# First attention of a two-layer macaron block: the products that sum the softmax totals, and the steps behind them, one loop unit later

## The chip, the cores and the metric

The kernel runs on one core of a Trainium2 chip. The metric is the device time of one execution in microseconds (us); of several runs the median counts. TensorE (PE in the profile) does matrix products, VectorE (DVE), ScalarE (ACT) and GpSimd (POOL) work elementwise, SyncE (SP) issues DMAs. Each engine works through its own queue in order, and engines wait for each other by semaphores.

## The reference

The input x is 2 batches of 1024 tokens of width 128. Six stages add to it in turn: a feed-forward layer with 4-bit weights and activations, attention A, the same feed-forward layer, a mixture-of-experts layer, attention B, and the mixture of experts again. The change touches only attention A:

```python
q, k, v = x @ Wq.T, x @ Wk.T, x @ Wv.T          # 16 heads of 64
sim = 50.0 * tanh((q @ k.T) * 64 ** -0.5 / 50.0)
sim = where(causal, sim, lowest)
attn = softmax(sim, axis=-1)                     # exp(sim) / its sum over the keys
x = x + (attn @ v) @ Wo.T
```

Since the tanh bounds sim to 50, the kernel takes no maximum: it computes exp(sim) as it is, multiplies it with v, and divides the result by the total of each row. How these totals reach the result is what the change is about.

## The kernel before

Two heads (a head pair, 128 rows) are worked on at a time, 8 head pairs in all. For each head pair p there are two slices, s = 2p for batch 0 and s = 2p + 1 for batch 1. A slice is cut into NU = 9 units of four 128 x 128 blocks of the causal half. The loop body `pair(p, more)` covers n = 0 to 17, that is the nine units of both slices; it stands once for p = 0, in a hardware loop for p = 1 to 6, and once for p = 7 (`span`). Every engine has its own `pair`, and the order in them is written out by hand.

For a unit n TensorE multiplies exp(sim) with V into the accumulator O in psum, in two halves (`multiply`, L860), and between these halves it computes the scores of unit n + 4 (`scores`, L841). ScalarE turns scores into tiles PR by tanh (L511) and exp (L516), two units at a time. GpSimd masks the diagonal blocks of PR (L488). Behind units 0 to 4 and 9 to 13 TensorE also projects Q, K and V of the next slice (L814, L818) into the psum banks J[0] and J[1], from which VectorE copies them to sbuf (`projected`: Q L639, K L641, V L643). When the nine units of a slice are multiplied, VectorE takes O out of psum (`take`, L650, at n = 1 and 10), and TensorE's first multiply of the next slice waits for that.

The totals go another way. VectorE (first head) and GpSimd (second head) add the PR tiles of a slice into an accumulator ACC as they come (`add_up`, L422 and L429; ACC of batch 0 is called XN in the profile, that of batch 1 ACC). After the slice the steps are these:

- `totals(s, b, value)` on TensorE (L873) multiplies ACC with ones into psum bank J[0]. It waits for all additions of the slice and, since J[0] is shared with the projections, for the V copies that empty it. Batch 1 of the pair before comes behind unit 5, batch 0 of this pair behind unit 14.
- `copy_totals(s)` on VectorE (L656) copies J[0] to DS.
- `spread(s)` on SyncE issues 4 DMAs from DS to RC (L443).
- `invert(s)` on VectorE (L660) takes the reciprocal of RC.
- `broadcast(s)` on SyncE stores RC in DRAM (L449) and reads it back to all partitions into RB, a part of XB in the profile (two DMAs, L453).
- `scale(s, b, p)` on VectorE (L666) multiplies the slice's output OT with RB. The output projection (`out`, L928) needs it at the end of the stage only.

In VectorE's loop body these steps stand behind `add_up`, `take` and `projected` of the same n. The Q copies stand at n = 1 and 10, the K copies at 3 and 12, the V copies at 5 and 14. In the last pair TensorE's loop ends at n = 13; the totals of its batch 0 and of the last slice are written out behind it. SyncE's queue has, for each pair, first the load of the next W (L459, once the projections of the slice are done), then spread and broadcast of slice 2p - 1, then those of slice 2p. The next side-0 projection waits until the totals of the slice two before are copied.

Of the kernel before, what the change touches and what calls it, by code (L numbers as in the profile page):

```python
# [323 lines left out]
def stage_front(nc, g, sem):  # L324
# [17 lines left out]
    with ExitStack() as tmp:  # L342
# [67 lines left out]
        def add_up(eng, s, b, u, h, done):  # L410

            if u == 0:
                wait(eng, z.totalled, s - 1)
            if ADDS[u]:
                unit_done(eng, s, u)
            for k, (n, to, first, second) in enumerate(ADDS[u]):
                into = split(ACC[b][:, h, :], n)[:, to, :]
                if second is None:
                    if h == 1:

                        eng.sem_inc(z.pooled, 1)
                    eng.tensor_copy(into, split(PR[first[0]][:, h, :], n)[:, first[1], :]).then_inc(done, 1)  # L422
                    continue
                if first is None:
                    wait(eng, done, ADDED[NU] * s + ADDED[u] + k)
                    old = into
                else:
                    old = split(PR[first[0]][:, h, :], n)[:, first[1], :]
                eng.tensor_tensor(into, old, split(PR[second[0]][:, h, :], n)[:, second[1], :], ALU.add).then_inc(done, 1)  # L429

        with nc.Block() as block:
# [201 lines left out]
            def _(dve):  # L633
                def projected(s, b, k):

                    dve.wait_ge(z.projected, 6 * s + k + 1)
                    half = slice(k % 2 * BANK, (k % 2 + 1) * BANK)
                    if k < 2:
                        dve.tensor_copy(Q[:, b, half], J[k % 2]).then_inc(z.query, 1)  # L639
                    elif k < 4:  # L640
                        dve.tensor_copy(K[:, b, half], J[k % 2]).then_inc(z.key, 1)  # L641
                    else:
                        dve.tensor_copy(V[:, b, 4 * (k % 2):4 * (k % 2) + 4, :].rearrange("p t f -> p (t f)"), J[k % 2]  # L643
                                        ).then_inc(z.value, 1)

                def take(s, b, p):

                    dve.wait_ge(z.multiplied, NU * s + NU)
                    for half in range(2):
                        dve.tensor_copy(heads_out(p, b, half * BANK, (half + 1) * BANK), O[:, half * BANK:(half + 1) * BANK]  # L650
                                        ).then_inc(z.taken, 1)

                def copy_totals(s):
                    dve.wait_ge(z.totalled, s + 1)
                    wait(dve, z.spread, 64 * s)
                    dve.tensor_copy(DS[:, :], J[0]).then_inc(z.copied, 1)  # L656

                def invert(s):
                    dve.wait_ge(z.spread, 64 * s + 64)
                    dve.reciprocal(RC[:, :, :], RC[:, :, :]).then_inc(z.inverted, 1)  # L660

                def scale(s, b, p):

                    dve.wait_ge(z.broad, 32 * s + 32)
                    dve.wait_ge(z.taken, 2 * s + 2)
                    dve.tensor_tensor(heads_out(p, b), heads_out(p, b), RB[:, :], ALU.mult).then_inc(z.scaled, 1)  # L666

                def pair(p, more):
                    first = isinstance(p, int) and p == 0
                    for n in range(2 * NU):  # L670
                        add_up(dve, 2 * p + n // NU, n // NU, n % NU, 0, z.summedA)
                        if n == 1 and not first:
                            take(2 * p - 1, 1, p - 1)
                        if n == 10:
                            take(2 * p, 0, p)
                        if n in (1, 3, 5):
                            projected(2 * p + 1, 1, n - 1)
                            projected(2 * p + 1, 1, n)
                        if n in (10, 12, 14) and more:
                            projected(2 * p + 2, 0, n - 10)  # L680
                            projected(2 * p + 2, 0, n - 9)
                        if n == 15:
                            copy_totals(2 * p)
                        if first:
                            continue
                        if n == 0:
                            invert(2 * p - 2)
                        if n == 3:
                            scale(2 * p - 2, 0, p - 1)
                        if n == 6:  # L690
                            copy_totals(2 * p - 1)
                        if n == 9:
                            invert(2 * p - 1)
                        if n == 12:
                            scale(2 * p - 1, 1, p - 1)

                def weights():
# [77 lines left out]
            def _(pe):  # L775
# [49 lines left out]
                def scores(s, b, u):  # L825
                    if u == 0:
                        pe.wait_ge(z.query, 2 * s + 2)
                        pe.wait_ge(z.key, 2 * s + 2)

                    wait(pe, z.clamped, NU * s + u - 1)  # L830
                    passed(s)
                    (near, far) = PIECES[u]
                    joined = len(near) == len(far) == 1 and near[0][0] == far[0][0]
                    for j, at, q, w in (near if joined else near + far):
                        for h in range(2):
                            for c in range(2):
                                into, of = S[(b + u) % 2][row[c], h, at:at + w], Q[row[h], b, q:q + w]
                                if joined:
                                    into = S[(b + u) % 2][row[c], h, :]
                                    of = split(Q[row[h], b, :], 2 * P)[:, q // (2 * P)::(far[0][2] - q) // (2 * P), :]  # L840
                                mm = pe.matmul(into, K[row[h], b, j * P + DH0 * c:j * P + DH0 * (c + 1)], of,  # L841
                                               start=True, stop=True, skip_group_check=True)
                    mm.then_inc(z.scored, 1)
# [33 lines left out]
                def pair(p, more):  # L877
                    begin = isinstance(p, int) and p == 0

                    def unit(n):  # L880

                        return 2 * p + n // NU, n // NU % 2, n % NU

                    for n in range(2 * NU if more else 2 * NU - AHEAD):
                        turned = n == 0 or n == NU and more
                        if turned:
                            if n:
                                pe.wait_ge(z.w, 16 * p + 32)
                            project(2 * p + 1 + n // NU, 1 - n // NU, 0, True)
                            scores(*unit(n + AHEAD))  # L890
                        multiply(*unit(n), n % 2 == 1, True)
                        if turned:
                            project(2 * p + 1 + n // NU, 1 - n // NU, 0, False)
                        else:
                            scores(*unit(n + AHEAD))
                        multiply(*unit(n), n % 2 == 1, False)
                        k = n % NU
                        if 1 <= k <= 4 and (n < NU or more):
                            project(2 * p + 1 + n // NU, 1 - n // NU, (k + 1) // 2, k % 2 == 1)
                        if n == 5 and not begin:  # L900
                            totals(2 * p - 1, 1, 4 * p + 4)
                        if n == 14:
                            totals(2 * p, 0, 4 * p + 6)
                    if not more:
                        pe.wait_ge(z.wo, 16)
                        for n in (14, 15, 16):
                            multiply(*unit(n), False, True)
                        totals(2 * p, 0, 4 * p + 4)
                        pe.wait_ge(z.clamped, 2 * NU * PAIRS)
                        out(0, 0, 1)  # L910
                        pe.wait_ge(z.halved, NU * last + NU - 1)
                        for n in (14, 15, 16):
                            multiply(*unit(n), False, False)
                        multiply(*unit(17), True, True)
                        out(0, 1, 2)
                        multiply(*unit(17), True, False)
# [1635 lines left out]
```

## Time and profile before

| | us |
|---|---|
| median of 3 runs | 1223.57 |
| lowest and highest | 1222.08, 1228.06 |
| the profiled execution | 1226.15 |
| its span | 1224.4 |
| TensorE busy in the span | 1129.5 (92%) |
| VectorE | 856.5 (70%) |
| ScalarE | 704.5 (58%) |
| GpSimd | 522.8 (43%) |

The span runs from the first to the last instruction in the trace. The first attention takes the time from about 60 to 456 us of it. Times in rows are microseconds from the start of the span, unless marked ns. In a timeline a row is a run of like instructions, merged: start, length, engine, line, operation, output and inputs, how many; in brackets is the idle time of the engine just before it and what released it. The ends of TensorE's instructions are modelled, so distances between starts are the safer reading.

### The profile page before, as it was taken

How to read it: one execution, taken by the hardware profiler on the slowest of the kernel's cores; microseconds unless marked ns; L12 is line 12 of the kernel's file. 1: busy time of each engine (PE TensorE's matmuls, PEld its weight loads, DVE VectorE, ACT ScalarE, POOL GpSimd, SP SyncE). 2: the span in 40 equal slices, each digit the busy share in tenths (PEclk: the TensorE clock that was granted, in tenths of full speed). 3: DMA queues.
4: the chain of work that ended last, by engine and by line, in shares of the span. 5: the costliest groups of instructions: out<-in, count | busy, mean ns of one | idle time of the engine just before them, and what ended most of it. 6: DMA issues, size and time to landing. Idle time of an engine off the chain costs nothing. (4 is left out here: it accounts for less than half of the span.)

```text
span 1224.4 us, 29054 instructions
## 1 busy us (share of the span) xinstructions
PE 1129.5 (92%) x10981; PEld 631.5 (52%) x10981; DVE 856.5 (70%) x1805; ACT 704.5 (58%) x915; POOL 522.8 (43%) x529
## 2 busy tenths in 40 slices
PE   3899999999999898879997999999999999788998
PEld 1456556566566585359983222222222222546996
DVE  6457767777777655874425899999999993585442
ACT  3587777777777525512225177777777778451220
POOL 0056666665666600337862114223322321035883
PEclk9799999999999998879999999999999999797999
DMA  4000110010010110516752211222222110223665
GB/s 128 1 9 20 27 42 18 24 42 18 24 42 19 27 30 1 176 59 173 197 94 89 75 43 54 62 58 57 61 57 54 54 51 18 92 88 116 182 171 122
DMA packets 60345, 81.83 MB, mean 67 GB/s; under 512 B 23488, under 2 KB 41284, under 8 KB 59612
## 3 DMA queue, kind: packets, MB, share of 16 engines
q1 hardware_dynamic: 48180, 70.54, 19.0%
q0 software_dynamic: 10880, 8.86, 4.9%
q8 instruction: 59, 0.97, 0.3%
q10 hardware_dynamic: 1192, 1.19, 0.3%
q14 instruction: 34, 0.28, 0.1%
HBM read 55.12 MB, written 15.72 MB: 58 GB/s over the span
## 5 line engine op out<-in xcount | busy, mean ns | idle before, releaser
L2020 ACT ACTIVATE at_PR<-psum 128x1024 f32<-128x1024 f32 x256 | 248.0, 1021 | 106.8 <-PE psum L2267 104.8
L2089 DVE TENSOR_REDUCE at_MX<-psum 128x1 f32<-128x512 f32 x468 | 298.2, 684 | 11.5 <-PE psum L2239 8.9
L511 ACT ACTIVATE PR<-psum 128x1024 f32<-128x1024 f32 x144 | 145.7, 1022 | 83.1 <-PE psum L841 74.7
L860 PE MATMUL psum<-PR,V 64*64 64x256 f32 (+1 forms) x2560 | 171.7, 357 | 5.1 <-issue 1.5
L841 PE MATMUL psum<-Q,K 64*64 64x512 f32 (+2 forms) x1792 | 151.5, 437 | 2.1 <-ACT PR L511 2.1
L860 PEld LDWEIGHTS psum<-PR,V 64*64 64x64 f32 x2560 | 96.9, 133 | 102.3 <-issue 90.4
L516 ACT ACTIVATE PR<-PR 128x1024 f32<-128x1024 f32 x144 | 143.8, 1051 | 0.0
L2284 PE MATMUL psum<-at_PR,at_VG 128*32 128x512 f32 x1024 | 136.2, 604 | 0.8 <-POOL at_PR L1957 0.8
L488 POOL TENSOR_SCALAR_AFFINE_SELECT PR<-PR 128x256 f32<-128x256 f32 (+1 forms) x80 | 57.1, 719 | 168.4 <-ACT PR L516 167.6
L1549 PE MATMUL psum<-moe_XGT,moe_WE 128*128 128x256 f32 x512 | 124.6, 388 | 0.2
L1957 POOL TENSOR_TENSOR at_PR<-at_PR,at_FAC 128x512 f32<-128x512 f32 x64 | 81.1, 1268 | 101.5 <-ACT at_PR L2020 101.5
L2239 PEld LDWEIGHTS psum<-at_KU,at_QU 64*128 64x128 bf16 x512 | 28.3, 92 | 171.5 <-DVE at_MX L2089 142.2
L1234 ACT ACTIVATE moe_GL<-psum 128x512 f32<-128x512 f32 x64 | 38.2, 597 | 131.0 <-PE psum L1549 131.0
L2239 PE MATMUL psum<-at_KU,at_QU 64*128 64x512 bf16 x512 | 99.7, 383 | 8.0 <-DVE at_MX L2089 1.8
L1549 PEld LDWEIGHTS psum<-moe_XGT,moe_WE 128*128 128x128 f32 x512 | 94.9, 195 | 11.1 <-issue 0.3
L1380 DVE TENSOR_TENSOR moe_H<-moe_GL,psum 128x512 f32<-128x512 f32 x64 | 44.0, 687 | 80.3 <-ACT moe_GL L1234 80.3
L2263 PE MATMUL psum<-at_QU,at_KU 64*128 64x512 bf16 x512 | 97.8, 377 | 1.7 <-DMA at_QL<-at_MR 1.3
L2267 PE MATMUL psum<-at_QL,at_KL 58*128 58x512 bf16 x512 | 97.8, 377 | 0.0
L1152 POOL DMA_INDIRECT moe_XG<-moe_rows_dram,moe_IDX x64 | 63.7, 996 | 52.4 <-DVE moe_IDX L1334 32.8
L841 PEld LDWEIGHTS psum<-Q,K 64*64 64x64 f32 x1792 | 68.2, 133 | 26.3 <-issue 10.5
L1159 POOL TENSOR_TENSOR moe_SG<-moe_SG,XN 128x512 f32<-128x512 f32 x16 | 20.3, 1270 | 123.7 <-ACT XN L1202 108.2
L1930 POOL CAST at_NMB<-at_NM 128x16 bf16<-128x16 f32 x16 | 3.2, 198 | 162.4 <-DVE at_NM L2095 162.4
(267 smaller groups left out, 1853.4 us busy)
## 6 DMA issues: line engine op xcount, KB each, us to landing
moe_WE<-in_c_We SPq DMA_DIRECT2D x32, 768.0 KB, 4.6
XB<-at_r_dram SPq DMA_DIRECT2D x32, 256.0 KB, 3.8
at_outs_dram<-at_OTS SPq DMA_DIRECT2D x15, 256.0 KB, 3.0
moe_rows_dram<-XNS SPq DMA_DIRECT2D x2, 1152.0 KB, 11.4
moe_spare_dram<-moe_zeros SPq DMA_DIRECT2D x2, 1024.0 KB, 13.9
moe_sum_dram<-XB SPq DMA_DIRECT2D x2, 1024.0 KB, 3.8
moe_SG<-moe_spare_dram SPq DMA_DIRECT2D x8, 256.0 KB
at_KU<-in_c_max_krows SPq DMA_DIRECT2D x16, 128.0 KB
```

The source lines that it names most:

```text
L511: act.activation(PR[u][:, :, :], S[(b + u) % 2][:, :, :], ACT.Tanh, scale=SCALE0 / CLAMP).then_inc(z.clamped, 1)
L516: act.activation(PR[u][:, :, :], PR[u][:, :, :], ACT.Exp, scale=CLAMP).then_inc(z.exped, 1)
L841: mm = pe.matmul(into, K[row[h], b, j * P + DH0 * c:j * P + DH0 * (c + 1)], of, start=True, stop=True, skip_group_check=True)
L860: mm = pe.matmul(O[row[h], q:q + w], V[rows, b, j, row[h]], PR[u][rows, h, at:at + w], start=(first and u == 0), stop=(not first and u == ...
L1549: mm = pe.matmul(ps[4 + 2 * m + h][:, j * CAP:(j + 1) * CAP], WE[:, e % DEEP, at:at + P], XGT[:, e % 2, :], start=True, stop=True)
L1957: pool.tensor_tensor(pr, pr, FAC[:, 4 * (s // 2):4 * (s // 2) + 4, :], ALU.mult).then_inc(z.factored, 1)
L2020: act.activation(PR[:, gu % PRS, 2 * r:2 * r + 2, :].rearrange("p h n -> p (h n)"), g.psum[:, 2 * r * BANK:(2 * r + 2) * BANK], ACT.Exp).t ...
L2089: dve.tensor_reduce(MX[:, c // 32 % 2, 8 * (c % 2) + 4 * pair + I % 4, khalf:khalf + 1], bank(("max", c))[:, :], AX, ALU.max).then_inc(z.r ...
L2239: mm = pe.matmul(bank(("max", c + h))[:, :], queries(QU[rows, s % UPPERS, pair, :])[:, I // 4, I % 4, :], KU[rows, s % UPPERS, pair, khalf ...
L2263: pe.matmul(ps[2 * j + a].rearrange("p (i n) -> p i n", n=P), KU[rows, s % UPPERS, j, J * P:(J + 1) * P], queries(QU[rows, s % UPPERS, j, ...
L2267: mm = pe.matmul(ps[2 * j + a].rearrange("p (i n) -> p i n", n=P), KL[rows, s % LOWERS, j, J * P:(J + 1) * P], queries(QL[rows, s % LOWERS ...
L2284: mm = pe.matmul(O[32 * h:32 * h + 32, :], VG[:, s % 2, J, h, :], PR[:, gu % PRS, h, :], start=(J == 0), stop=(J == BT - 1), skip_group_ch ...
```

## The change

`totals` moves from behind unit 5 to behind unit 6, and from behind unit 14 to behind unit 15. In VectorE's body the copy of the totals, the inversion and the scaling each move one position later: 15 to 16 and 6 to 7, 0 to 1 and 9 to 10, 3 to 4 and 12 to 13. SyncE's DMAs keep their order and follow through their semaphores. The code of the tail is the same.

```diff
@@ on VectorE, in pair()
-                        if n == 15:
+                        if n == 16:
                             copy_totals(2 * p)
                         if first:
                             continue
-                        if n == 0:
+                        if n == 1:
                             invert(2 * p - 2)
-                        if n == 3:
+                        if n == 4:
                             scale(2 * p - 2, 0, p - 1)
-                        if n == 6:
+                        if n == 7:
                             copy_totals(2 * p - 1)
-                        if n == 9:
+                        if n == 10:
                             invert(2 * p - 1)
-                        if n == 12:
+                        if n == 13:
                             scale(2 * p - 1, 1, p - 1)
@@ on TensorE, in pair()
-                        if n == 5 and not begin:
+                        if n == 6 and not begin:
                             totals(2 * p - 1, 1, 4 * p + 4)
-                        if n == 14:
+                        if n == 15:
                             totals(2 * p, 0, 4 * p + 6)
```

## Rows read from the trace of the kernel before

**Rows 1.** The page, its first line: the span.
```profile
span 1224.4 us, 29054 instructions
```

**Rows 2.** TensorE's waits and groups, 60 to 441 us (wait: total, times, longest; group: busy, mean ns | idle before).
```profile
PE psum L873 <- DVE V L643: 8.2, 7, 1.2
...
L860 PE MATMUL psum<-PR,V 64*64 64x256 f32 (+1 forms) x2560 | 171.7, 357 | 5.1 <-issue 1.5 <-POOL PR L488 1.1 <-DVE OT L650 1.0
...
L928 PE MATMUL psum<-WO,OT 128*128 128x128 f32 x128 | 15.0, 277 | 0.0
L873 PE MATMUL psum<-XN,ones 128*32 128x512 f32 x64 | 8.5, 605 | 7.2 <-DVE V L643 7.2
L873 PE MATMUL psum<-ACC,ones 128*32 128x512 f32 x64 | 8.5, 604 | 1.0 <-DVE V L643 1.0
```

**Rows 3.** Timeline of TensorE around three totals products.
```profile
329.33 0.64 PE L860 MATMUL psum<-PR,V 64*64 64x128 f32 x16
331.17 1.07 PE L873 MATMUL psum<-XN,ones 128*32 128x512 f32 x8 [1.20 <-DVE V L643]
...
333.51 1.04 PE L860 MATMUL psum<-PR,V 64*64 64x256 f32 x16
...
335.23 1.04 PE L860 MATMUL psum<-PR,V 64*64 64x256 f32 x16
...
352.84 0.65 PE L860 MATMUL psum<-PR,V 64*64 64x128 f32 x16
353.42 1.06 PE L873 MATMUL psum<-ACC,ones 128*32 128x512 f32 x8
...
399.87 1.07 PE L873 MATMUL psum<-ACC,ones 128*32 128x512 f32 x8 [1.04 <-DVE V L643]
```

**Rows 4.** Timeline of the other engines around the product at 331.17.
```profile
324.27 2.00 DVE L666 TENSOR_TENSOR OT<-OT,XB 128x1024 f32 x1
325.14 1.39 POOL L488 TENSOR_SCALAR_AFFINE_SELECT PR<-PR 128x256 f32<-128x256 f32 x1
...
329.84 1.27 DVE L643 COPY V<-psum 128x512 f32<-128x512 f32 x2
...
330.10 0.41 POOL L488 TENSOR_SCALAR_AFFINE_SELECT PR<-PR 128x256 f32<-128x256 f32 x1 [0.73 <-ACT PR L516]
...
332.39 0.69 DVE L656 COPY DS<-psum 128x512 f32<-128x512 f32 x1
...
333.00 1.70 DVE L429 TENSOR_TENSOR ACC<-ACC,PR 128x512 f32<-128x512 f32 x2
...
333.92 1.02 ACT L511 ACTIVATE PR<-psum 128x1024 f32<-128x1024 f32 x1 [3.06 <-PE psum L841]
...
337.79 1.29 DVE L650 COPY OT<-psum 128x512 f32 x2 [0.81 <-PE psum L860]
```

**Rows 5.** Timeline of VectorE and TensorE where a take came late.
```profile
154.61 0.25 DVE L660 RECIPROCAL RC<-RC 128x16 f32<-128x16 f32 x1 [1.64 <-DMA RC<-DS]
154.86 1.29 DVE L650 COPY OT<-psum 128x512 f32 x2
...
156.50 0.66 PE L860 MATMUL psum<-PR,V 64*64 64x256 f32 x8 [1.05 <-DVE OT L650]
```

**Rows 6.** Timeline of VectorE in the first half of a pair.
```profile
340.99 1.29 DVE L639 COPY Q<-psum 128x512 f32<-128x512 f32 x2 [1.92 <-PE psum L814]
...
347.81 1.21 DVE L666 TENSOR_TENSOR OT<-OT,XB 128x1024 f32 x1
...
357.31 1.36 DVE L422 COPY ACC<-PR 128x256 f32<-128x256 f32 x1 [0.30 <-POOL PR L488]
...
360.00 1.29 DVE L650 COPY OT<-psum 128x512 f32 x2 [0.78 <-PE psum L860]
```

**Rows 7.** Timeline of VectorE in the tail of the attention.
```profile
434.27 0.25 DVE L660 RECIPROCAL RC<-RC 128x16 f32<-128x16 f32 x1 [1.54 <-DMA RC<-DS]
...
440.57 1.23 DVE L666 TENSOR_TENSOR OT<-OT,XB 128x1024 f32<-128x1024 f32 x1 [6.04 <-DMA XB<-at_r_dram]
```

## The prediction, made before the change was run

> **What bounds the kernel now.** I looked first at the page, to see whether one engine carries the span, then at TensorE's groups and waits in the stretch of the first attention (60 to 441 us), because every instruction that the change touches lies there, then at the timelines of TensorE, VectorE, ScalarE and GpSimd around a totals product, and last at the tail. The span is 1224.4 us [rows 1]. In the attention TensorE is all but never idle: the multiplies of L860 waited 5.1 us in that stretch, and the totals products of L873 waited 7.2 us in front of the batch-0 ones and 1.0 us in front of a batch-1 one [rows 2]. So TensorE sets the pace, and the totals products are its largest wait: 8.2 us, 7 times, at most 1.2 us, each released by VectorE's V copy (L643) [rows 2]. The reader should see the cause in the code: the totals go into psum bank J[0], which the value projection of the same unit slots still occupies until VectorE has copied V away, in the same loop position (5 or 14) where the totals are issued.
>
> One pair in numbers. The product behind unit 14 starts 1.84 us after the multiply ahead of it (329.33 to 331.17), the one behind unit 5 only 0.58 us (352.84 to 353.42) [rows 3]. The wait thus costs 1.84 - 0.58 = 1.26 us, a little over the 1.20 in brackets. The V copies that end it run to 329.84 + 1.27 = 331.11 us [rows 4]. In the last pair the product behind unit 5 waited too, 1.04 us [rows 3].
>
> **The change part by part.**
>
> *Totals one unit later.* Nothing is added or removed: 8 profiled matmuls per product; 14 of the 16 products move (seven behind unit 5, seven behind unit 14; those of the last pair's batch 0 and of the last slice stand in the tail's code and stay). A unit without a projection takes 1.72 us (333.51 to 335.23 [rows 3]), and the next unit after 5 and after 14 is such a one. Without the wait unit 15 begins at 329.33 + 0.58 = 329.91, and the totals would follow at 329.91 + 1.72 = 331.63, which is 0.52 us behind the end of the V copies at 331.11. So the wait goes: 6 times 1.26 = 7.6 us (6 is 7.2 / 1.20), and 1.0 us in the last pair. What is late next there? TensorE's own work, units 15 and 16, whose PR tiles are ready: ScalarE stood idle for 3.06 us at 333.92, waiting for the scores of unit 19 that TensorE issues in unit 15 [rows 4]. They now come 2.26 us earlier (the wait and the 1.0 us product no longer precede them), so ScalarE gains distance and isn't the new bound.
>
> *The inversion one unit later.* At loop position 0 the reciprocal stood ahead of the take of O at position 1, and TensorE's first multiply of a slice waits for that take. Once, at 154.61, the reciprocal waited 1.64 us for its spreading DMA; the take came behind it at 154.86, and TensorE lost 1.05 us at 156.50 [rows 5]. Now the reciprocal comes behind the take and the two Q copies, where nobody on TensorE waits for it. That gives 1.0 us, and at most 1.0, as it shows only once. The copy of the totals moves too, so the spread has as many units as before.
>
> *What then becomes tight: the broadcast.* SP's DMAs move with the steps: four spreads behind the copy, one store and two broadcasts behind the inversion. SP's queue keeps its order, and the load of the next W still waits for the projections and not for these. From the end of a reciprocal to the scaling that waits for its broadcast it took 440.57 - (434.27 + 0.25) = 6.05 us in the tail, where the wait was the DMA's [rows 7]. Inside the loop the reciprocal now ends near the end of the Q copies, 340.99 + 1.29 + 0.25 = 342.53, so the broadcast is there at 348.6. The scaling at position 4 follows the K copies (347.81, where it stands today) and two adds of about 0.85 each (half of 1.70): 349.5 [rows 4, 6]. It has 0.9 us to spare. If it hadn't, VectorE would hold the V copies up, which themselves have 0.5 us before TensorE notices. Cost taken: 0; bounds: 0 and the lateness of the next paragraph.
>
> *Scaling one unit later.* The same instruction takes 1.21 us in one place (347.81) and 2.00 in the other (324.27) [rows 4, 6]; it leaves a position with two copies for one with none, but it still stands ahead of the V copies, so their time is the same sum of the same terms in another order. Between bounds of 0.8 us earlier (1.21 for 2.00) and 1.4 us later (a GpSimd mask that took 1.39 instead of 0.41, as seen beside the scaling [rows 4]), I take no change, as the K copies ahead and the work between stay the same.
>
> That mask and that scaling were both slow at the same time: 1.39 for 0.41, 2.00 for 1.21 [rows 4, 6]. The Trainium skill, SBUF — State Buffer, in the section on who interferes with whom, says that a VectorE instruction with two SBUF inputs contends with a GpSimd instruction that reads SBUF, and that the one that begins first holds the other for its full length; these rows agree. By that rule alone the moved scaling may meet another GpSimd instruction and come out either way, and the sum would be that of the first rival.
>
> *Copy of the totals one position later.* Behind unit 15 TensorE ends earlier and VectorE has over 2 us of room before the take at 337.79 [rows 4]. Behind unit 6 it is tighter: product at 353.42 + 1.72 = 355.14, copy 1.22 us after its start as at 332.39 against 331.17, so 356.36, next instruction 0.6 later, one add of 0.85, then the slice's first copy of 1.36 (357.31) to 359.2; the take is due at 360.00 [rows 3, 4, 6]. It has 0.8 us to spare: cost 0, but this is the place of the slower rival.
>
> *Last pair and tail.* All of it is behind TensorE's order and shifts along; the batch-0 copy now stands behind one more add and costs at most 0.85 us of VectorE's time. Its taker, the output products of L928, waited 0.0 us in all [rows 2], although the last scaling itself came 6.04 us late by its own wait [rows 7]. Cost 0.
>
> **The sum**: 7.6 + 1.0 + 1.0 = 9.6 us. The profiled execution took 1226.15 us (1224.4 its span, 1.75 around it), so it would be 1216.6; the median of the runs shown is 2.6 us lower, 1223.57, and 1223.57 - 9.6 = 1214.0. A difference under 0.5% (6.1 us) can't be told from none here.
>
> **The rivals.**
>
> 1. *The wait comes back in part* (13%). The V copies come later than 331.63 because the scaling, or an add, meets a GpSimd instruction. For it: only 0.52 us of room, against 0.79 us by which one scaling differs from another. Against it: VectorE works without a pause from the scaling to the V copies, with the same instructions. If they come 1.39 us later, 1.39 - 0.52 = 0.87 us return, 6 times, 5.2 us: gain 4.4, time 1219.2.
>
> 2. *The wait only changes its name* (5%). Freed of it, TensorE runs into ScalarE or the masks in units 15 to 17, as the pace of 1.72 us per unit is the fastest of the pair. The 3.06 us of idle time on ScalarE speak against it [rows 4]. The same time would follow if L643 is only the last releaser by name. Then 1223.6, no change.
>
> 3. *Slower* (4%): the take is late at the middle of each pair. The copy of the totals at position 7 waits for TensorE's unit 6, and queued behind it are an add, the copy into ACC and the take, for which TensorE's multiply of unit 9 waits. It decides from 0.82 us of added lateness on; beyond, each microsecond is TensorE's, 7 times. To be slower by 6.1 us it must eat 15.7 us, so 2.2 each, 3.1 us of lateness in all. Contention made single instructions here 0.8 to 1.0 us longer, and three stand in the queue, so it is possible but needs them all. At 2.5 each: 1223.57 - 9.6 + 17.5 = 1231.5.
>
> **How the numbers follow.** The forecast has 78%: 1214.0, give or take 1.5 (the takes delayed by a DMA vary from run to run, and the V copies may miss by tenths). Rival 1 ends it upwards at 1219.2, so the range goes from 1211.5 to 1220.0; it leaves out rivals 2 and 3. Faster by over 0.5% (below 1217.5): the forecast and a light rival 1, 0.79. Within: most of rival 1 and rival 2, 0.17. Slower: 0.04.
>
> **What would show it.** Right: L873 no longer released by L643; the start of a batch-0 product 0.6 us behind the multiply ahead of it, and each pair of the loop 1.26 us shorter; no wait for L650 but the tail's; the scaling not waiting for XB inside the loop; VectorE's wait for the totals near zero behind unit 15. Wrong: new waits of L860 on L650 at the middle of a pair (rival 3), of L841 or L860 on ScalarE or GpSimd in units 15 to 17 (rival 2), L873 still behind L643 (rival 1), or the gain given back after 441 us.

## The result, and the profile after

The changed kernel took 1212.88 us (median of 5 runs, 1210.92 to 1214.27) beside 1223.47 us for the kernel before (5 runs). The ratio is 0.9898 with a 95% interval of 0.9875 to 0.9921: faster by about 1%. The same kernel beside the kernel before a second time, on another occasion, gave 0.9927 (0.9905 to 0.9949). The profiled execution took 1214.02 us, its span 1212.3.

TensorE's waits in the attention, 60 to 441 us, in the changed kernel (total us, times, longest). Both waits that the change was about are gone from the list [rows 2]; what is left stands in the last pair and at the start.
```profile
PE psum L860 <- issue: 1.5, 1, 1.5
PE psum L860 <- POOL PR L488: 1.1, 1, 1.1
PE psum L841 <- ACT PR L511: 0.8, 1, 0.8
```

The timeline of TensorE around a batch-0 product and the slice boundary behind it, in the changed kernel; it answers to [rows 3].
```profile
321.48 0.63 PE L860 MATMUL psum<-PR,V 64*64 64x256 f32 x8
322.04 1.07 PE L873 MATMUL psum<-XN,ones 128*32 128x512 f32 x8
...
327.39 1.04 PE L841 MATMUL psum<-Q,K 64*64 64x512 f32 x8
328.56 0.66 PE L860 MATMUL psum<-PR,V 64*64 64x256 f32 x8
```
The product now starts 0.56 us behind the multiply ahead of it, where it was 1.84.

The other engines at the same place, again the changed kernel; it answers to [rows 4].
```profile
313.48 1.29 DVE L641 COPY K<-psum 128x512 f32<-128x512 f32 x2 [0.91 <-PE psum L814]
...
316.35 2.29 DVE L666 TENSOR_TENSOR OT<-OT,XB 128x1024 f32 x1
318.56 1.76 DVE L429 TENSOR_TENSOR ACC<-ACC,PR 128x512 f32<-128x512 f32 x1
320.25 1.27 DVE L643 COPY V<-psum 128x512 f32<-128x512 f32 x2
321.45 2.95 DVE L429 TENSOR_TENSOR ACC<-ACC,PR 128x512 f32<-128x512 f32 x2
324.32 0.68 DVE L656 COPY DS<-psum 128x512 f32<-128x512 f32 x1
...
326.92 1.29 DVE L650 COPY OT<-psum 128x512 f32 x2 [0.94 <-PE psum L860]
330.13 1.29 DVE L639 COPY Q<-psum 128x512 f32<-128x512 f32 x2 [1.92 <-PE psum L814]
331.33 0.24 DVE L660 RECIPROCAL RC<-RC 128x16 f32<-128x16 f32 x1
```
The V copies end at 320.25 + 1.27 = 321.52, which is 0.52 us ahead of the product, the very room that the prediction had worked out. They are as late as before: from the first K copy to the first V copy it takes 6.77 us here and 6.78 in the kernel before (323.06 to 329.84). VectorE got no faster; TensorE only no longer asks at the wrong moment. The scaling took 2.29 us here, as long as any in the kernel before, and it costs nothing. The reciprocal stands behind the take and the Q copies and didn't wait. One scaling in the loop waited for XB, 0.28 us at 116.34, and the product behind it came without a wait all the same.

**Where the time went.** The page's span mixes three things, so I measure one stretch in every kernel: from the first side-0 projection in the loop to the first instruction of the output product. Here are its ends, first in the kernel before, then in the changed one.
```profile
64.17 1.07 PE L814 MATMUL psum<-XT,Wqkv 64*64 64x512 f32 x8
...
420.38 1.98 PE L923 MATMUL psum<-X,ident 128*128 128x512 f32 x4
```
```profile
60.70 1.07 PE L814 MATMUL psum<-XT,Wqkv 64*64 64x512 f32 x8
...
407.12 1.98 PE L923 MATMUL psum<-X,ident 128*128 128x512 f32 x4
```
The stretch went from 356.21 to 346.42 us: 9.79 less. The front ahead of it was 3.47 us shorter, the rest behind it 1.16 us longer (804.02 and 805.18). Together -12.1, the difference of the spans. Starts of neighbouring runs account for the 9.79 to a tenth: from the multiply ahead of it to each of the 14 products that moved, the distances sum to 16.70 us before and 7.89 after, 8.81 less; at the twelve slice boundaries of the loop, from scores to first multiply, to 14.95 and 13.89, 1.06 less, of which 0.91 is the one late take of [rows 5] (2.08 before, 1.17 after).

### The profile page after: what moved, and what is told of

Same layout as the page of the kernel before. It is cut to its first block and busy times, and to the rows that moved or that the text cites. A ratio compares the mean times of both kernels' runs of the same rounds, so it can differ in the third digit from the quotient of the medians.

```text
span 1212.3 us, 29054 instructions
## 1 busy us (share of the span) xinstructions
PE 1127.0 (93%) x10981; PEld 628.2 (52%) x10981; DVE 862.3 (71%) x1805; ACT 705.0 (58%) x915; POOL 522.3 (43%) x529
## 3 DMA queue, kind: packets, MB, share of 16 engines
q10 hardware_dynamic: 1192, 1.19, 0.3%
## 5 line engine op out<-in xcount | busy, mean ns | idle before, releaser
L860 PE MATMUL psum<-PR,V 64*64 64x256 f32 (+1 forms) x2560 | 172.0, 357 | 4.0 <-issue 1.5
L860 PEld LDWEIGHTS psum<-PR,V 64*64 64x64 f32 x2560 | 96.3, 133 | 98.9 <-issue 88.8
L488 POOL TENSOR_SCALAR_AFFINE_SELECT PR<-PR 128x256 f32<-128x256 f32 (+1 forms) x80 | 54.2, 682 | 155.1 <-ACT PR L516 154.8
```

Of the source, the lines that this page charges most:

```text
L860: mm = pe.matmul(O[row[h], q:q + w], V[rows, b, j, row[h]], PR[u][rows, h, at:at + w], start=(first and u == 0), stop=(not first and u == ...
```

## The experiments

All timed runs had the kernel before beside them on the same chip. The stretch is worth most, since it repeats: 346.42 in the profile of the changed kernel, 346.40 in its second one. TensorE's mean granted clock over it reads 1.00 in all thirteen profiles. Each stretch is from one profile. Three of the expectations (inversion and scaling only, batch 0 only, two units) count it from the first scores, at 66.06 us in the kernel before and 1.89 us later: their 354.3, 345.7 and 344.5 are 356.2, 347.6 and 346.4 here.

| kernel | stretch, us | ratio (95% interval) |
|---|---|---|
| before | 356.21 | 1 |
| changed | 346.42 | 0.9898 (0.9875 to 0.9921) |
| changed, again | 346.40 | 0.9927 (0.9905 to 0.9949) |
| products and their copy only | 368.23 | 1.0147 (1.0131 to 1.0164) |
| inversion and scaling only | 355.37 | 0.9992 (0.9976 to 1.0009) |
| batch-0 steps only | 348.08 | 0.9930 (0.9912 to 0.9947) |
| batch-1 steps only | 354.54 | 0.9989 (0.9971 to 1.0007) |
| two units instead of one | 346.59 | 0.9939 (0.9922 to 0.9955) |
| before, scaling behind V copies | 347.51 | 0.9942 (0.9920 to 0.9963) |
| changed, scaling behind V copies | 346.40 | 0.9922 (0.9900 to 0.9945) |
| changed, written out | 342.21 | 0.9897 (0.9875 to 0.9920) |
| changed, written out, scaling behind V copies | 342.21 | 0.9924 (0.9904 to 0.9944) |
| before, written out | 359.56 | 1.0073 (1.0050 to 1.0096) |

**Only the products and their copy moved.** Against the changed kernel:
```diff
-                        if n == 1:
+                        if n == 0:
                             invert(2 * p - 2)
-                        if n == 4:
+                        if n == 3:
                             scale(2 * p - 2, 0, p - 1)
...
-                        if n == 10:
+                        if n == 9:
                             invert(2 * p - 1)
-                        if n == 13:
+                        if n == 12:
                             scale(2 * p - 1, 1, p - 1)
```


> Totals behind units 6 and 15 and their copy at positions 16 and 7, as in the change; inversion and scaling stay where they were (0 and 9, 3 and 12). Theory (the inversion's move is needed, since the spread then lands behind the moment at which the take is due): spread plus inversion end about 0.9 us behind that moment (copy ends 333.5 in the frame of the batch-0 product, spread 3.6 us, reciprocal 0.25, take due 336.5), at 14 slice boundaries, 12.6 us lost against 8.6 won: 1227, waits of L860 on L650 of about 1 us, 14 times. Rival (the totals' wait was all there was): 8.6 us faster than before, 1215, no waits on L650. For the front of the program (start to the scores at 66.06 before, 62.59 after): the theory that its TensorE clock differs from execution to execution expects either value in any kernel; the rival that the changed order itself makes it shorter expects 62.6.

The totals' wait was gone, and the kernel was 1.5% slower. TensorE's waits in this kernel, and VectorE and TensorE at one boundary:
```profile
PE psum L860 <- DVE OT L650: 18.8, 12, 2.5
```
```profile
338.53 2.95 DVE L429 TENSOR_TENSOR ACC<-ACC,PR 128x512 f32<-128x512 f32 x2
341.41 0.68 DVE L656 COPY DS<-psum 128x512 f32<-128x512 f32 x1
...
345.72 0.25 DVE L660 RECIPROCAL RC<-RC 128x16 f32<-128x16 f32 x1 [2.66 <-DMA RC<-DS]
345.97 1.29 DVE L650 COPY OT<-psum 128x512 f32 x2
```
```profile
339.12 1.06 PE L873 MATMUL psum<-XN,ones 128*32 128x512 f32 x8
...
347.66 0.66 PE L860 MATMUL psum<-PR,V 64*64 64x256 f32 x8 [2.15 <-DVE OT L650]
```
The mechanism is as expected: the spread lands 3.63 us behind the end of the copy (342.09 to 345.72), the reciprocal waits for it, the take stands behind the reciprocal, and TensorE waits for the take. The size was off. I had taken the copy to follow the product's start by 1.22 us; here it is 341.41 - 339.12 = 2.29, because VectorE is still at its adds. That is 1.07 more in the batch-0 half, and with it 12.6 us expected, at 14 boundaries, became 18.8 at 12. So a step that looks like bookkeeping, the inversion one position later, is what makes the rest of the change possible.

**Only inversion and scaling moved.** Against the kernel before:
```diff
-                        if n == 0:
+                        if n == 1:
                             invert(2 * p - 2)
-                        if n == 3:
+                        if n == 4:
                             scale(2 * p - 2, 0, p - 1)
...
-                        if n == 9:
+                        if n == 10:
                             invert(2 * p - 1)
-                        if n == 12:
+                        if n == 13:
                             scale(2 * p - 1, 1, p - 1)
```


> Only inversion and scaling one position later (0 to 1, 9 to 10, 3 to 4, 12 to 13); totals and their copy as before. Theory (the V copies are as late as before, since the scaling still stands ahead of them): L873 goes on waiting for L643 some 8 us in all, 7 times; the stretch from the first projection of the loop to the first output product stays within 1.5 us of the 354.3 of before; time 1222.5, within 0.3% of before. Rival (the moved scaling frees VectorE ahead of the V copies and the moved totals matter less): L873 waits under 5 us, time 1218 to 1220. Front as in the run before this one: either value, or 62.6 by the rival.

```profile
PE psum L873 <- DVE V L643: 8.3, 7, 1.2
```
The totals' wait stayed as it was (8.3 us, 7 times), the late take went, and the stretch was 0.84 us shorter. The rival fell.

**Only one batch's steps moved.** For batch 0, against the kernel before:
```diff
-                        if n == 15:
+                        if n == 16:
                             copy_totals(2 * p)
...
-                        if n == 0:
+                        if n == 1:
                             invert(2 * p - 2)
-                        if n == 3:
+                        if n == 4:
                             scale(2 * p - 2, 0, p - 1)
...
-                        if n == 14:
+                        if n == 15:
                             totals(2 * p, 0, 4 * p + 6)
```


> The steps of the batch-0 slices moved as in the change (totals behind unit 15, copy at 16, inversion at 1, scaling at 4); those of the batch-1 slices stay (5, 6, 9, 12). Theory: the six waits of 1.26 us go (7.6 us), the one of about 1.0 in the last pair stays, the late take at 156.50 goes: 8.6 us faster than before, 1215, stretch about 345.7; TensorE's period of a pair is that of the change. Rival (batch-1 steps held VectorE up as well, and their move gave part of the gain): under 7 us faster, and waits of L873 behind unit 14 or 15 that are still there in part.

For batch 1, against the kernel before:
```diff
-                        if n == 6:
+                        if n == 7:
                             copy_totals(2 * p - 1)
-                        if n == 9:
+                        if n == 10:
                             invert(2 * p - 1)
-                        if n == 12:
+                        if n == 13:
                             scale(2 * p - 1, 1, p - 1)
...
-                        if n == 5 and not begin:
+                        if n == 6 and not begin:
                             totals(2 * p - 1, 1, 4 * p + 4)
```


> Only the steps of the batch-1 slices moved (totals behind unit 6, copy at 7, inversion at 10, scaling at 13). Theory (the halves add up: the change took 9.8 us from the stretch, batch 0 alone 8.1): stretch 354.5, 1.7 us less than before, the six waits of 1.20 us on L643 still there; time 1222, not told from before. Rival (the scaling at 13 instead of 12 makes the V copies later, hidden in the change because the product no longer waits for them): the six waits grow, by up to 0.9 us each, stretch 356 to 361.

TensorE's wait for the V copies, first with batch 0 moved, then with batch 1 moved:
```profile
PE psum L873 <- DVE V L643: 1.1, 1, 1.1
```
```profile
PE psum L873 <- DVE V L643: 7.2, 6, 1.2
```
Batch 0 brought 8.13 us (8.6 expected), batch 1 1.67, and 8.13 + 1.67 = 9.80 is the whole. The six waits and the one part cleanly.

**Two units instead of one.** Against the changed kernel:
```diff
-                        if n == 16:
+                        if n == 17:
                             copy_totals(2 * p)
...
-                        if n == 1:
+                        if n == 2:
                             invert(2 * p - 2)
-                        if n == 4:
+                        if n == 5:
                             scale(2 * p - 2, 0, p - 1)
-                        if n == 7:
+                        if n == 8:
                             copy_totals(2 * p - 1)
-                        if n == 10:
+                        if n == 11:
                             invert(2 * p - 1)
-                        if n == 13:
+                        if n == 14:
                             scale(2 * p - 1, 1, p - 1)
...
-                        if n == 6 and not begin:
+                        if n == 7 and not begin:
                             totals(2 * p - 1, 1, 4 * p + 4)
-                        if n == 15:
+                        if n == 16:
                             totals(2 * p, 0, 4 * p + 6)
```


> All steps two units later than before instead of one (totals behind units 7 and 16, copy at 8 and 17, inversion at 2 and 11, scaling at 5 and 14). Theory (once the totals don't wait nothing more is to be had, and VectorE just reaches the take of the middle in time): the same as the change, 1213 to 1214, stretch 344.5 give or take 1. Rival (the slower rival of the prediction: the copy of the totals, held up by TensorE's unit, makes the take at the middle of a pair late): L860 waits on L650 in the middle of pairs, 0.5 to 2 us each, 7 times: 1217 to 1227.

The middle of a pair on VectorE in this kernel:
```profile
306.34 0.69 DVE L656 COPY DS<-psum 128x512 f32<-128x512 f32 x1 [0.81 <-PE psum L873]
306.95 0.28 DVE L422 COPY ACC<-PR 128x256 f32<-128x256 f32 x1
308.26 1.29 DVE L650 COPY OT<-psum 128x512 f32 x2 [1.03 <-PE psum L860]
```
The stretch is that of the change (346.59). Although the copy of the totals comes a unit later still, the take waits for TensorE and not the other way round. The queue that the slower rival feared isn't long: the copy into ACC took 0.28 us here, not the 1.36 of [rows 6]. The median, 1219.67 us, lies where the rival had put it, but beside 1226.24 for the kernel before on that chip; what the rival rests on, waits of L860 on L650, isn't in the list.

**The same wait cured from the other side.** The kernel before, with the scaling alone moved behind the V copies:
```diff
-                        if n == 3:
+                        if n == 5:
                             scale(2 * p - 2, 0, p - 1)
...
-                        if n == 12:
+                        if n == 14:
                             scale(2 * p - 1, 1, p - 1)
```


> The kernel before with one edit: the two scalings move from positions 3 and 12 to 5 and 14, where they stand behind the V copies; totals, their copy and the inversion stay. Theory (the V copies were late because the scaling stood ahead of them on VectorE, so this cures the same wait from the other side): waits of L873 on L643 gone or under 1 us in all, the V copies now released by TensorE (L818). But the totals' copy stands behind the scaling now, so the spread lands about 0.4 us after the batch-0 take is due: some 2 to 3 us of waits on L650 come in. Stretch from the first projection of TensorE's loop to the first output product 348 to 350 (356.2 before, 346.4 with the change), 6 to 8 us faster than before. Rival (J[0] frees late because VectorE is short of time as a whole): L873 keeps at least 4 us of waits, stretch above 352.

```profile
314.78 1.29 DVE L641 COPY K<-psum 128x512 f32<-128x512 f32 x2 [0.94 <-PE psum L814]
...
319.98 1.29 DVE L643 COPY V<-psum 128x512 f32<-128x512 f32 x2 [0.58 <-PE psum L818]
321.19 1.22 DVE L666 TENSOR_TENSOR OT<-OT,XB 128x1024 f32 x1
322.32 0.89 DVE L429 TENSOR_TENSOR ACC<-ACC,PR 128x512 f32<-128x512 f32 x1
323.13 0.68 DVE L656 COPY DS<-psum 128x512 f32<-128x512 f32 x1
```
This names the cause of the wait. With the scaling out of the way VectorE stands ready for V, 5.20 us behind the K copies and not 6.78, and the wait of L873 is gone from the list. One move on one engine brings 8.7 of the 9.8 us (347.51, below the 348 to 350 expected); what is missing is the late take. The late takes that I expected weren't there but for one of 0.9 us (L860 behind L650): the scaling took 1.22 us and the add behind it 0.89, less than I had allowed. In the changed kernel the same move does nothing:

> The changed kernel with the scalings at 5 and 14 instead of 4 and 13. Theory (in the change no wait of TensorE is left that the place of the scaling could end): stretch 346.4 within 0.4, the time of the change. Rival (VectorE's slack still counts): 1 us or more less, or, if the scaling behind the V copies delays the copy of the totals, more.

Its stretch is 346.40. Where TensorE doesn't wait, VectorE's room is worth nothing.

**The changed kernel again.**

> The changed kernel once more, beside the kernel before on this chip, to part what the change brings from what differs between executions. Theory (the change is worth the 9.8 us of the attention stretch and nothing elsewhere): ratio 0.992, interval from about 0.990 to 0.994, stretch 346.4 within 0.3; front and rest may lie anywhere between those seen (first projection at 60.7 to 64.9, rest 804 to 809). Rival (the ratio of the first comparison, 0.9898, is the change's own): 0.990 or under again.

Stretch 346.40, ratio 0.9927: what the change brings is the stretch. It began its first projection at 61.96 and had 805.14 us of rest.

**Loop written out.** The changed kernel, the six middle pairs without a loop on every engine:
```diff
-                with eng.Fori(1, PAIRS - 1) as p:
+                for p in range(1, PAIRS - 1):
                     body(p, True)
```


> The changed kernel with the six middle head pairs written out instead of looped over, so that every semaphore wait has a constant. In the loop TensorE's first multiply of a slice starts 0.35 us behind the end of the take, in the last pair, written out, 0.10 us. Theory (the difference is the waiting against a register's value): 0.25 us less at each of 12 boundaries, 3 us less in the stretch, 343.5, time about 1210. Rival (the loop costs nothing, and the longer code brings stalls of its own while instructions are fetched): stretch 346.4 or more.

TensorE and VectorE at a boundary of this kernel:
```profile
285.64 1.04 PE L841 MATMUL psum<-Q,K 64*64 64x512 f32 x8
286.50 0.61 PE L860 MATMUL psum<-PR,V 64*64 64x256 f32 x8
```
```profile
285.03 1.29 DVE L650 COPY OT<-psum 128x512 f32<-128x512 f32 x2 [0.81 <-PE psum L860]
```
From scores to first multiply it takes 0.86 us, against 1.17 in the looped kernel (327.39 to 328.56); the multiply starts 0.18 us behind the end of the take, not 0.35. Over the 12 boundaries the distance from scores to multiply sums to 10.30 us, where it was 13.89: 3.6 of the 4.2 us gained (3 expected). The first boundary of the last pair, which isn't in the loop, had 0.86 and 0.18 in the looped kernel too; the 0.10 of the expectation is from the pair's middle. Whether the wait against a register's value is the reason, or something else that the loop brings, wasn't tried apart. That every such wait costs this much isn't so: in the kernel before the waiting product started 0.06 us behind the end of the V copies inside the loop (331.11 to 331.17), and 0.15 us behind it with the loop written out. The same with the scaling behind the V copies:

> The changed kernel with the middle pairs written out and the scalings at 5 and 14. Theory (as in the looped kernel, nothing waits for the scaling): stretch 342.2 within 0.4, and 12 to 14 us faster than before in its runs, the fastest so far with the written-out one. Rival (with shorter boundaries VectorE's slack begins to count): 341 or less.

The stretch is the same, 342.21, and 14.0 us below that of the kernel before, the shortest measured. The median isn't: 1213.59 beside 1222.99, 9.4 us less and not the 12 to 14 expected. In total times the written-out kernels (0.9897, 0.9924) aren't told from the looped change (0.9898, 0.9927): 4 us is less than the intervals allow. They are better by their stretch only.

**The kernel before, written out.** The same edit on the kernel before.

> The kernel before with the six middle head pairs written out instead of looped over. Theory (loop and totals' wait are separate costs that add up): it gains the 4.2 us that writing out gained on the changed kernel (346.4 to 342.2), so stretch 352.0, and keeps 8 us of waits of L873 on L643; boundary gaps on TensorE 0.86 instead of 1.17 us. The change is then worth 9.8 us on the written-out kernel too. Rival (with the boundaries shorter VectorE has less time, and the V copies come later still): L873 waits over 10 us, stretch 353 or more.

Here my theory failed: the kernel became slower, 1.0073, stretch 359.56, and L873 waits twice as long:
```profile
PE psum L873 <- DVE V L643: 14.2, 13, 1.2
```
The products behind unit 5 wait now too. VectorE and GpSimd in the first half of a pair tell why. Two fences are of this kernel, the next two of the kernel before:
```profile
303.13 1.29 DVE L641 COPY K<-psum 128x512 f32<-128x512 f32 x2 [1.76 <-PE psum L814]
304.33 1.70 DVE L666 TENSOR_TENSOR OT<-OT,XB 128x1024 f32<-128x1024 f32 x1
305.95 1.50 DVE L429 TENSOR_TENSOR XN<-PR 128x256 f32<-128x256 f32 x1
...
309.61 1.27 DVE L643 COPY V<-psum 128x512 f32<-128x512 f32 x2
```
```profile
304.22 2.96 POOL L429 TENSOR_TENSOR XN<-XN,PR 128x256 f32<-128x256 f32 x2
```
```profile
346.60 1.29 DVE L641 COPY K<-psum 128x512 f32<-128x512 f32 x2 [1.67 <-PE psum L814]
...
348.94 0.95 DVE L429 TENSOR_TENSOR XN<-PR 128x256 f32<-128x256 f32 x1
```
```profile
347.90 3.14 POOL L429 TENSOR_TENSOR XN<-XN,PR 128x256 f32<-128x256 f32 x2
```
In the kernel before, VectorE's scaling (347.81 [rows 6]) begins 0.09 us ahead of GpSimd's first add into XN and takes 1.21 us; it is the add that is held, 1.71 us for itself. Written out, the same add begins 0.11 us ahead (304.22 against 304.33) and takes 0.73 us, and the scaling takes 1.70 and VectorE's add behind it 1.50 instead of 0.95: 1.04 us more. From K copy to V copy it is 6.48 us instead of 5.46, and each product behind unit 5 starts 1.65 us behind its multiply instead of 0.58. Over the 14 products that is 6.1 us more (22.83 for 16.70), while the boundaries took 2.6 us less (12.38 for 14.95); four of the boundaries still had 1.19 to 1.63 us in place of 0.86, for which the trace names no releaser, and why stays open. The last pair of the kernel before, which has never been in the loop, shows the same, with GpSimd's add 0.08 us ahead (393.06):
```profile
393.14 1.73 DVE L666 TENSOR_TENSOR OT<-OT,XB 128x1024 f32<-128x1024 f32 x1
394.79 1.50 DVE L429 TENSOR_TENSOR XN<-PR 128x256 f32<-128x256 f32 x1
```
There was the seventh wait, of 1.04 us [rows 3]. The Trainium skill, SBUF — State Buffer, section on who interferes with whom, says that a VectorE instruction with two SBUF inputs contends with a GpSimd one that reads SBUF, that the shared port pair is an exclusive lock, and that issue order decides who blocks. These rows agree: a shift of 0.2 us between the engines turned the order round. What shifted them wasn't found, and no kernel here moved one of the two instructions alone. On the written-out kernel the change is thus worth 359.56 - 342.21 = 17.4 us and not 9.8.

## Why the prediction was right or wrong

**The mechanism and the sum were right.** Forecast 9.6 us: 7.6 for six waits, 1.0 for the last pair's, 1.0 for the late take. Measured in the stretch: 9.79, as 8.81 in front of the products (7.7 for the six, 1.1 for the last pair's) and 1.06 at the boundaries; by halves, 8.13 and 1.67. The median, 1212.88, is 1.1 below the predicted 1214.0 and inside the range, and a gain of over 0.5% had 79%.

**The range's lower end was wrong.** By the ratio the time is 1223.57 x 0.9898 = 1211.1 (1208.3 to 1213.9 by its interval), below the 1211.5. The step that failed is "give or take 1.5 (the takes delayed by a DMA vary from run to run, and the V copies may miss by tenths)": it looked for scatter inside the stretch, where there is hardly any (0.02 us between two profiles), and put at nothing, without a reason, the parts of the program that the change doesn't touch. There the profiles differ by more than the 1.5: the front ahead of the stretch took 60.68 to 66.19 us, the rest behind it 803.7 to 809.4. The five runs of the changed kernel lie 3.35 us apart and the five of the kernel before 6.5. By the second ratio, 0.9927, the time is 1214.6, 0.6 from the forecast; so the miss by 0.4 us says little against the sum, and the first median, 1.1 us from the forecast, little for it; the stretch tests it. The front first. TensorE's same instructions there, before and after the change, in the order of these two fences:
```profile
35.74 2.08 PE L216 MATMUL psum<-X,ident 128*128 128x512 f32 x2
37.75 2.07 PE L217 MATMUL psum<-bias,ones 1*128 1x512 f32 x2
```
```profile
35.54 1.12 PE L216 MATMUL psum<-X,ident 128*128 128x512 f32 x2
36.59 1.12 PE L217 MATMUL psum<-bias,ones 1*128 1x512 f32 x2
```
```profile
30.00:50.00 20.00, 16.97 (x60) 10.07 (x59) 11.59 (x44) 8.93 (x19) 0.00 (x0) 0.74 0.00 0
```
```profile
30.00:50.00 20.00, 16.34 (x69) 8.40 (x67) 11.62 (x44) 9.89 (x21) 0.00 (x0) 0.91 0.00 0
```
The last two fences are the windows view from 30 to 50 us, before and after (the last but two columns is the granted clock): 0.74 and 0.91 of full speed, that is more and less time at the lower of the two levels, 1.2 and not 2.4 GHz. Up to 35 us the two executions run within 0.03 us of each other; by the first projection they are 3.47 us apart. Over all profiles the front sorts by its mean granted clock: 60.68 and 60.70 us at 0.97, 60.94 to 61.99 at 0.94, 64.10 to 64.88 at 0.89, 65.55 and 66.19 at 0.87. It is no effect of the change: the first projection began at 60.94 and 61.99 with the products unmoved, and at 64.14 and 64.88 with all or some of them moved. What decides the clock in an execution stays open; it takes more values than the two that the first expectation allowed. In the 17 runs of the kernel before beside the first four experiments the time fell from 1232.17 us at a mean clock of 0.968 and 1231.24 at 0.965 to 1221.43 at 0.976, though not strictly (1228.69 at 0.973). A second part, unexplained, is the rest behind the stretch: 808.2 to 809.4 us in four profiles taken together, 803.7 to 805.2 in all others, and the mean clock of all but one reads the same there, 0.96. A ratio of five runs to five carries both; the intervals of 0.9898 and 0.9927 overlap (0.9905 to 0.9921).

**Rival 1**, the wait back in part: it didn't come. The room of 0.52 us held, but not because the terms stayed: the scaling took 2.29 us for 2.00 and the last add 1.76 for 1.66, the first add 1.20 for 0.62 and the second 0.51 for 1.38, and the sum came out the same to 0.01 us (6.77 for 6.78). The prediction had counted on the same terms in another order; that changed terms give the same sum no run explains, and the hit on 0.52 is in part luck. On the slow scaling of [rows 4] the rows that it showed lack the one that held it, a mask of 1.09 us that began 0.17 us ahead, at 324.10; the mask of 1.39 us there began behind the scaling and was held in turn. **Rival 2**, another engine in its place: no. The scores of unit 19 came earlier as said, and ScalarE's idle time of 3.06 us in front of unit 19 shrank to 0.63. **Rival 3**, the take late in the middle: no, but the place was well chosen. The kernel with only the products and their copy moved shows what a late take costs, 18.8 us over 12 waits, more than all that the change brings.

**Two steps were right in result and off in size.** The copy of the totals had "over 2 us of room" in the batch-0 half. It follows the product's start there by 324.32 - 322.04 = 2.28 us, since VectorE is still at its adds, and not by the 1.22 of the other half (1.23 measured there); the take had 0.94 us to spare. In the other half, the tight one, it had 1.06 and not 0.8. And the late take of [rows 5] was called worth 1.0 "and at most 1.0"; beside the unmoved inversion that is so, but the inversion's move is no extra of 1 us: without it the products' move loses 12 us instead of winning.

## What to carry to other kernels

A wait that one engine names (TensorE, for a bank) can be cured at either end: ask later, as here, or let the work that stands ahead of the release go behind it, which alone brought 8.7 of the 9.8 us. When a step of a chain through several engines moves later, move the steps that wait for it too, and look above all at the one that stands ahead of something urgent in its queue: left in place, the inversion turned a gain of 9.8 us into a loss of 12. For a change of under 1%, compare the stretch that it touches between profiles with the same granted clock in it: that repeated to 0.02 us, while the time of the whole program moved by more than the effect.

## What the runs showed of the hardware that wasn't expected

Where VectorE's scaling and GpSimd's add began 0.1 us apart, the order went with 1.04 us on VectorE (scaling and next add 1.21 and 0.95 us, or 1.70 and 1.50). In the kernel before, looped or written out, the outcome was the same in each of the six middle pairs, and in the written-out one six further waits came with it. At 0.02 us apart the order no longer tells: a mask of GpSimd that began that much ahead of the scaling took 1.50 us and the scaling 1.21 in one kernel (changed, written out, 122.14 and 122.16), 0.41 and 1.46 in another (changed, 383.26 and 383.28). A loop written out made one kernel 4.2 us faster and the other 3.35 us slower. In the changed kernel, the loop cost TensorE 0.28 to 0.31 us at each of its 12 slice boundaries.
